# DLRM tower on one core: who issues and converts the head tables' loads, and a re-laid order of 96 moving units a block

## The reference

```python
e = jnp.stack([tbl_0[ids[:, 0]], ..., tbl_39[ids[:, 39]]], axis=1)   # 2048 x 40 x 64
vi, vj = x[:, i_idx, :], x[:, j_idx, :]                              # the 780 pairs i < j
z = jnp.einsum('bpe,bpe->bp', jnp.einsum('bpd,pde->bpe', vi, W), vj)
h = jnp.concatenate([z, dense_ctx], axis=1)                          # 780 + 16
h = jnp.maximum(h @ W_top1 + b_top1, 0.0)                            # 512
h = jnp.maximum(h @ W_top2 + b_top2, 0.0)                            # 256
y = h @ W_top3
```

## Time and profile before

| | before |
|---|---|
| median of 3 runs | 1236.23 us (1236.14 to 1239.3) |
| the profiled execution | 1235.82 us |
| its span, first to last instruction | 1233.9 us |
| busy in it: PE, DVE, ACT, POOL | 1189.6, 1064.7, 976.7, 778.2 us |
| VectorE products (units) | 800 |
| R units summed by V, A, P | 102, 234, 48 |
| mean DMA rate | 66 GB/s |

### The profile page before, as it was taken

One profiled execution on the slowest core, in us unless ns is written; L12 is line 12 of the kernel. 1 busy time (PEld: TensorE's weight loads), 2 busy tenths in 40 slices (PEclk: granted clock), 3 DMA queues, 4 the chain that ended last, 5 costly groups with the idle time before them and its releaser, 6 DMA issues.

```text
span 1233.9 us, 22918 instructions
## 1 busy us (share of the span) xinstructions
PE 1189.6 (96%) x5656; PEld 429.3 (35%) x5656; DVE 1064.7 (86%) x973; ACT 976.7 (79%) x7625; POOL 778.2 (63%) x1032
## 2 busy tenths in 40 slices
PE   4899998999999999999999999999999999999999
PEld 1332332333333333333333333433333334333333
DVE  4789999999987979999989979789989898989960
ACT  0149859999868889999959769999959687899971
POOL 7888882467765555787755656678766565545420
PEclk9999999999999999999999999999999999999999
DMA  4243222222222222222223222222222222212100
GB/s 152 72 143 71 69 69 55 59 72 68 71 63 60 64 61 69 69 67 68 68 64 77 62 58 64 62 64 67 69 63 69 59 68 64 61 48 54 55 5 1
DMA packets 65868, 80.92 MB, mean 66 GB/s; under 512 B 14772, under 2 KB 41396, under 8 KB 65608
## 3 DMA queue, kind: packets, MB, share of 16 engines
q1 hardware_dynamic: 44064, 55.14, 15.3%
q0 software_dynamic: 19456, 19.96, 9.2%
q10 hardware_dynamic: 2216, 4.36, 1.0%
HBM read 79.40 MB, written 0.01 MB: 64 GB/s over the span
## 4 chain that ended last, share of the span: by engine, by line
PE 91%; DVE 3%; ACTq 3%; issue 2%; ACT 1%; DVEq 0%
PE u_ps L921 31%; PE u_ps L917 28%; PE z_ps L938 16%; PE turn_ps L969 7%; PE turn_ps L889 3%; PE turn_ps L882 2%; PE turn_ps L979 2%; ACTq L1163 2%; PE u_ps L969 1%; DVE rprod_V L1056 1%; DVE rprod_A L1056 1%; DVE zb L1075 1%; ACTq L1161 1%; DVE fprod L1069 1%; PE u_ps L979 1%
## 5 line engine op out<-in xcount | busy, mean ns | idle before, releaser
L1118 ACT ACTIVATE rprod_A<-rprod_A 128x64 f32<-128x64 f32 x3744 | 895.8, 243 | 57.8 <-DVE rprod_A L1056 56.7
L826 POOL DMA_INDIRECT rows<-in_tbl,ids_all x608 | 576.0, 947 | 326.5 <-PE u_ps L921 114.3
L1118 ACT ACTIVATION_READ_ACCUMULATOR rprod_A<-rprod_A 128x1 f32 x3744 | 707.9, 189 | 0.1
L1069 DVE TENSOR_TENSOR fprod<-u_ps,x 128x1024 f32<-128x1024 f32 x416 | 492.9, 1214 | 36.1 <-PE u_ps L921 36.1
L921 PE MATMUL u_ps<-x,wf_ring 64*128 64x512 f32 x1664 | 428.5, 612 | 11.5 <-DVE rprod_V L1056 6.9
L917 PE MATMUL u_ps<-wr_ring,x 64*128 64x512 f32 x1536 | 394.8, 613 | 5.0 <-DVE rprod_V L1056 4.7
L1056 DVE TENSOR_TENSOR rprod_A<-u_ps,rows 128x1024 f32<-128x1024 f32 x234 | 281.8, 1216 | 71.4 <-PE u_ps L917 71.1
L921 PEld LDWEIGHTS u_ps<-x,wf_ring 64*128 64x128 f32 x1664 | 145.4, 185 | 242.8 <-issue 152.6
L917 PEld LDWEIGHTS u_ps<-wr_ring,x 64*128 64x128 f32 x1536 | 132.7, 186 | 221.7 <-issue 129.6
L938 PE MATMUL z_ps<-fprod,ones 128*32 128x512 f32 x1664 | 206.8, 598 | 0.0
L846 POOL TENSOR_TENSOR rprod_P<-rprod_P 128x512 f32<-128x512 f32 (+4 forms) x240 | 145.6, 607 | 77.1 <-DVE rprod_P L1056 61.4
(11 more groups left out here) (35 smaller groups left out, 187.4 us busy)
## 6 DMA issues: line engine op xcount, KB each, us to landing
wf_ring<-in_w_standing SPq DMA_DIRECT2D x208, 128.0 KB
wr_ring<-in_w_moving SPq DMA_DIRECT2D x96, 256.0 KB
rows<-in_tbl,ids_all POOLq DMA_INDIRECT x608, 2.5
mlp_sb<-in_mlp SPq DMA_DIRECT2D x1, 2308.0 KB, 9.8
mlp_sb<-in_tbl ACTq DMA_DIRECT2D x6, 250.0 KB
rows<-in_first_ids ACTq DMA_DIRECT2D x4, 250.0 KB
rprod_P<-in_first_ids ACTq DMA_DIRECT2D x4, 250.0 KB
mlp_sb<-in_tbl ACTq DMA_DIRECT2D x2, 312.5 KB
```

Source lines behind the costliest of these rows:

```text
L826: nc.gpsimd.indirect_dma_start(rows[:, v % ROW_SLOTS, s, par * DIM:(par + 1) * DIM], None, tables[f], bass.IndirectOffsetOnAxis(ap=ids_all ...
L1069: nc.vector.tensor_tensor(fprod[:, f % FPROD_SLOTS], u_ps[:, bank:bank + 2, :], other, ALU.mult).then_inc(prods_done, 1)
L1118: op = nc.scalar.activation(of[:, j, :], of[:, j, :], ACT.Copy, accum_out=sums_at(u, j, 1))
```

## The change

1. **Loads.** The loads of the 8 hot tables and of their ids go from ScalarE's queue to SP's. SP issues the ids of all gathers, then the loads of tables 0 to 3, then the first four chunks of standing weights, then tables 4 to 7, then the moving weights. The ids go to 128 partitions and not to 125; a table's load is cut into two, 112 and 13 partitions. Ids and tables have semaphores of their own.
2. **Ids as floats.** ScalarE converts each 128x512 ids tile in place from int32 to float32 (`convert_ids`, 8 instructions). VectorE's build waits for the converted ids and no longer for the table; TensorE waits for the table.
3. **The order.** Quads 2 and 3 of the fields have 5 and 7 moved columns and not 4 and 8 (still 24 chunks, 96 units a block). The costs and limits of the planner change. The turn of a chunk of row sums ("zr") may be placed within its own block, when its sums are done, and need not stand before layer 1 in the next one. What the planner makes of it: R units summed by V, A, P go from 102, 234, 48 to 89, 228, 67 (by block V: 33, 23, 24, 22 to 32, 25, 20, 12; P: 7, 12, 13, 16 to 11, 15, 17, 24). Block 0 takes its first P sum behind 126 of the 128 gathers of duos 4 to 19.

The core of the diff (the costs of the planner are numbers of a table; a line or two of it stands here):

```diff
-MOVED = [0, 4, 4, 8, 8]
+MOVED = [0, 4, 5, 7, 8]
+HOT_LOADS = [slice(0, 112), slice(112, 125)]
...
-LEAD, LEAST, ROWS_LEAD = 4, 1, 5
+LEAD, LEAST, ROWS_LEAD = 6, 1, 4
-A_MOST, P_MOST = 1.5, 1
+A_MOST, P_MOST = 1, 1
...
 def tail_of(b):
-    return ([("zr", b, c) for c in range(ZR)] + [("l1", b, m) for m in range(M1)] +
-            [("l2", b, m) for m in range(M2)] + [("l3", b, 0)])
+    return [("l1", b, m) for m in range(M1)] + [("l2", b, m) for m in range(M2)] + [("l3", b, 0)]
...
         for b in range(NB):
             base, f, r = DUOS * b, 0, 0
+            mlp += [("zr", b, c) for c in range(ZR)]
...
+            def load_table(h):
+                f, at = HOT_FIELDS[h], HOT_AT[h]
+                sp.dma_start(hot_ids[h].bitcast(I32),
+                             first_ids[h:h + 1, :].partition_broadcast(P)).then_inc(hot_ids_in[h], 16)
+                table = tables[f].rearrange("(p r) d -> p (r d)", p=HOT_PARTS)
+                for parts in HOT_LOADS:
+                    sp.dma_start(mlp_sb[parts, at:at + DIM * HOT_SPLIT[h]], table[parts, :]).then_inc(hot_in[h], 16)
+            for h in range(4):
+                load_table(h)
             for c in range(WF_SLOTS):
                 load_standing(c)
+            for h in range(4, 2 * HOT):
+                load_table(h)
...
-                            pe.wait_ge(hot_in[h], 2 * 16)
+                            pe.wait_ge(hot_in[h], 16 * len(HOT_LOADS))
...
-                    dve.wait_ge(hot_in[h], 2 * 16)
+                    dve.wait_ge(hot_ids_known, h + 1)
...
+            def convert_ids(n):
+                for h in range(2 * n, 2 * n + 2):
+                    act.wait_ge(hot_ids_in[h], 16)
+                    nc.scalar.copy(hot_ids[h], hot_ids[h].bitcast(I32)).then_inc(hot_ids_known, 1)
...
+                if v + 2 < HOT:
+                    convert_ids(v + 2)
...
-            for h, f in enumerate(HOT_FIELDS):
-                at = HOT_AT[h]
-                act.dma_start(hot_ids[h][0:HOT_PARTS, :],
-                              first_ids[h:h + 1, :].partition_broadcast(HOT_PARTS)).then_inc(hot_in[h], 16)
-                act.dma_start(tables_sb[:, at:at + DIM * HOT_SPLIT[h]],
-                              tables[f].rearrange("(p r) d -> p (r d)", p=HOT_PARTS)).then_inc(hot_in[h], 16)
+            for n in range(2):
+                convert_ids(n)
```

More of the change, by code:

```diff
@@ L198 @@
 T_GATHER, T_ROWS, T_FOLD = 1.25, 2.5, 3.3
-T_PACE, PACE_OVER, AHEAD_OF = 1.6, 4, 1.0
+T_PACE, PACE_OVER, AHEAD_OF = 1.6, 6, 1.0
 LAG_PE, LAG_DVE, LAG_ACT, LAG_POOL = 0.225, 0.15, 0.09, 0.08
 T_FIRST = 4.3
-T_HOT, T_BUILD, T_TABLE, T_TABLES = 0.423, 0.35, 5.5, 2.8
-LEAD, LEAST, ROWS_LEAD = 4, 1, 5
-STALL, GAP = 0.05, 0.2
+T_HOT, T_BUILD, T_TABLE, T_TABLES = 0.423, 0.35, 6.0, 1.6
+LEAD, LEAST, ROWS_LEAD = 6, 1, 4
+STALL, GAP = 0.05, 0.5
 MLP_GAP, MLP_PACE = 4, 14
-AHEAD, BEHIND = 2, 6
-A_MOST, P_MOST = 1.5, 1
+AHEAD, BEHIND = 1, 6
+A_MOST, P_MOST = 1, 1
 def tail_of(b):
-    return ([("zr", b, c) for c in range(ZR)] + [("l1", b, m) for m in range(M1)] +
-            [("l2", b, m) for m in range(M2)] + [("l3", b, 0)])
+    return [("l1", b, m) for m in range(M1)] + [("l2", b, m) for m in range(M2)] + [("l3", b, 0)]
 class Plan:
@@ L477, in step_ready @@
         if what == "zr":
+            if len(self.r_units) < NR * b + min(NR, SUBS * (P // FOLD) * (n + 1)):
+                return None
             for u in self.r_units:
@@ L564, in run @@
                     len(self.f_units) + 1 - FPROD_SLOTS >= NF * sums[0][0] + GROUP * sums[0][1])
-                must_step = mlp and any(ev[0] in ("zr", "l1") for ev in mlp) and sums and (
+                must_step = any(ev[0] in ("zr", "l1") and ev[1] < b for ev in mlp) and sums and (
                     sums[0][1] >= K_GROUPS * (Z_SPARE + 1) - 1)
@@ L592, in run @@
                     if sb == b - 1 and sg == GROUPS - 1:
-                        mlp = tail_of(sb)
+                        mlp[len(mlp) - ZR:len(mlp) - ZR] = tail_of(sb)
                 elif what == "duo":
@@ L613, in run @@
             self.do_sums(*s)
-        for ev in tail_of(NB - 1):
+        for ev in mlp + tail_of(NB - 1):
             self.do_step(ev)
@@ L691, in dlrm_tower @@
         hot_ids = [(rows[:, h, :, :].rearrange("p s c -> p (s c)") if h < 4
-                    else rprod["P"][:, (h - 4) // 2, (h - 4) % 2, :]).bitcast(I32) for h in range(2 * HOT)]
+                    else rprod["P"][:, (h - 4) // 2, (h - 4) % 2, :]) for h in range(2 * HOT)]
         y_row = h1_sb[0:1, 0, :]
@@ L706, in dlrm_tower @@
         hot_in = [sem(f"hot_in{h}") for h in range(2 * HOT)]
+        hot_ids_in = [sem(f"hot_ids_in{h}") for h in range(2 * HOT)]
+        hot_ids_known = sem("hot_ids_known")
         rows_known = sem("rows_known")
```

## The result

The changed kernel takes 1227.1 us (median of four runs, 1225.2 to 1228.4) and the kernel before 1236.3 beside it: a ratio of 0.9915, interval 0.9901 to 0.9928. That is 9.2 us faster, where 17.3 were forecast. The time lies inside the range of 1207 to 1230 and outside the forecast's own range of 1213 to 1224. The profiled execution took 1225.2 (span 1223.4), the quickest of the four. The other three took 1226.5 to 1228.4, at mean granted clocks of TensorE of 0.996, 0.994 and 0.994 where the profiled one had 0.997.

What follows compares the result with a forecast made beforehand. It took TensorE to bound the kernel, 91% of the chain of waits, with its idle time in the first 64 us. Head -13.5, row sums -1.1, end -2.7 gave -17.3, so 1219 us; own range 1213 to 1224, wider range 1207 to 1230.

Steps and rivals of the forecast that it cites:

- Head: loads: Table loads at the kernel's start: on SP's queue they run at 237 GB/s, so table 1 is there at 9.0 us.
- The slow bound: Table loads in the head at 143 GB/s: table 1 at 13 us, four us later, the head's gain only -9.5 us.
- Head: ScalarE: ScalarE in the head: its 16 load issues go, conversions of 0.59 us come, and the 5.25 us wait for a copy goes.
- Head: builds: VectorE's builds in the head stay at 0.53 us each, held up mutually with POOL; float ids bring nothing.
- The low end: Head with builds of 0.27 us: TensorE's own chain then decides, ending at 44.9 us, -16.2 us.
- Head: sum: The head ends at 47.6 us, by VectorE's chain, and not at 61.1: -13.5 us.
- Does block 0 follow?: Block 0 behind the head: gathers land before duos 7 and 11 are turned, so gathers were put at nothing.
- Row sums: VectorE's row sums: one fewer at 98 to 238 us, where a sum costs its whole 1.13 us; -1.1 us.
- the other twelve: The other twelve sums VectorE loses: put at nothing, bound 13.6 us to the good.
- the four rivals: Order gives more, 1209 (0.22); head half mended, 1223 to 1229 (0.13); loads still blocked, 1228 (0.06); POOL late, 1240 (0.04).
- rival 2: The head is only half mended, its loads coming at the slow rate: about 1223 to 1229 us, chance 0.13.
- The end: Before the last layer 1: two of three rounds of row-sum turns go, -2.7 us, or -1.1 at the least.

Runs made afterwards that it cites:

- head_load125: head with each hot table in one load of 125 partitions, not 112 and 13, and its ids on 125 partitions; 1228.3 us, ratio 0.9918 to the kernel before.
- head: The changed kernel's new head (loads, float ids) with the planner and order of the kernel before; 1223.9 us, ratio 0.9891 to the kernel before.
- head_short_pause: head with POOL's pause between block 0's gathers as a memset of 8 columns, not 256; 1220.7 us, ratio 0.9858 to the kernel before.
- mixed_again: Second run of mixed, on a chip of usual speed; 1218.1 us, ratio 0.9846 to the kernel before.
- replan: The changed kernel with one planner condition mended: a chunk turn is forced only by sums of the present block; 1222.6 us, ratio 0.9886 to the kernel before.
- zr2_later: The changed kernel with the third chunk turn of blocks 0 to 2 moved to just before the next turn; 1231.9 us, ratio 0.9959 to the kernel before.
- head_tail_again: Second run of head_tail, on a chip of usual speed; 1221.6 us, ratio 0.9871 to the kernel before.
- order: The kernel before with the changed kernel's planner, so the new order with the old head; 1240.5 us, ratio 1.0026 to the kernel before.
- head_tail: head with the last block's first two chunk turns placed among the units; on the slow chip alone, ratio 0.9931 to the kernel before there.
- head_int: head with integer ids and no conversions on ScalarE; on the slow chip alone, ratio 0.9956 to the kernel before there.
- mixed: replan with the planner's six old constants in block 0 alone; on the slow chip, ratio 1.0092 to the kernel before there.
- zr2_b0: The changed kernel with block 0's third chunk turn alone moved behind the block's last sums; slow chip alone, 1363.1 us, ratio 1.0228 to the kernel before.

## Why the forecast was right in sign and too large

1. **Head: loads.** Right in the rate, and not quite in what waits for what. Table 1 was to be there at 9.0, of which the 1 us for the end of a load has no row. A build waits for converted ids and no longer for the table: its ids are there by 8.54, and the second build starts at 9.18. The profile puts TensorE's first weight load from table 1, at 9.82, down to the table, so it was there by then; this cost nothing, as the builds set the pace. The slow bound, 143 GB/s and a table four us later, is what head_load125 measures: 141 GB/s, that weight load at 13.80 and not at head's 9.87, the second build 3.2 us later and the last layer 1 4.4.
2. **Head: ScalarE.** Right. A conversion takes 0.62 where 0.59 was taken, and the copy that came at 33.41 comes at 19.78.
3. **Head: builds.** Right in the term (0.54 for 0.53) and in its cause, POOL's pause. Float ids bring nothing at this pace: 18.74 us for 35 builds with int32 against 18.76. The Trainium skill (Advanced Engine Details and Errata, VectorE Performance Modes) names no type among the conditions of the two-port mode, and the trace agrees. The low end, TensorE's own chain to 44.9, is what head_short_pause reaches with 44.7.
4. **Head: sum.** 48.4 for 47.6, -12.7 us for -13.5. Short by 0.8, and all of it at the end: the products before the last two builds start at 43.97, as forecast (44.0). The last two builds take 1.09 us and not 0.87, and the last two steps (four matmuls) wait 1.39 us and take 1.46, so the head ends 1.1 us behind the last build where one step of 0.45 was put.
5. **Does block 0 follow?** Right. Duo 7 turns at 64.75 (64.0 forecast) and TensorE waits for gathers three times, by 1.2 us in all and 0.5 at most; head keeps the 12.7 to the end.
6. **Row sums.** This step failed, in block 0. One V sum fewer was to give 1.1 us, and "the other twelve" and the turns nothing. Block 0 lost 2.1 us in the changed kernel instead (3.2 in replan, with the same list there and a slow clock). I had compared counts over 100 units and not how the order around them falls. mixed_again shows that the planner's six constants for block 0 decide it: with them as before, block 0 loses nothing behind product 25. The single mechanism is open. The twelve sums in blocks 1 to 3 did bring little: from product 225 to 800 the changed kernel gains 2.2 us.
7. **What the sum left out.** Nothing in it priced the border of blocks. It had the turns earlier "among units where VectorE has the pace", and the order showed one directly behind the last unit whose row sums it needs. Price: 4.8 us, of which 1.9 is the slow clock (5.61 for 3.70); zr2_later, with the turn elsewhere, does not pay it. It is the largest missing term. None of the four rivals named it; rival 2's interval holds the time, but its cause (slow loads) was not there. That 1227.1 lies inside 1207 to 1230 is therefore partly luck: the width was given for other reasons.
8. **The end.** -2.6 for -2.7 in the rounds; the bound of -1.1 net, with the turns at 0.8 each, is closer to what head_tail_again shows, 1.5 net with 0.6 each.

The sum as measured in the profiled runs: -12.6 + 2.1 + 4.8 - 2.2 - 2.6 = -10.5, and the spans differ by 10.5. The medians give 9.2. The three slower runs have the lower mean clocks, so more slow clock is the likely reason for the difference; no trace of them is kept. Where the order has neither fault, in mixed_again, layer 1 is 17.7 us earlier and the kernel takes 1218.1, near the forecast's sum by slightly other terms: 13.0 by product 25, 0.1 in the rest of block 0, 1.9 in blocks 1 to 3 and 2.7 at the end. Its granted clock is 1.00 throughout, which also helps it.

## What to carry to other kernels

Price an order of instructions by its places and not by its counts: at each border ask of every instruction that needs a whole block's result how much work the engine that makes that result still has ahead of it, because everything queued behind the instruction waits too, and the clock can fall with it. Run the halves of a change apart first; head and order showed in two runs that the one gave more than the whole and the other cost. Where two engines' short instructions lengthen each other, shorten the one that does no work: the pause of 8 columns gave 3.8 us at the last layer 1, and the conversion of the ids cost about 1 at the first product.

## What the runs showed of the hardware that was not expected

- **One of the chips is much slower for this kernel.** On it the kernel before took 1332.5 us, and head_tail 0.9931, head_int 0.9956, mixed 1.0092 and zr2_b0 1.0228 of that. The head is the same there to 0.1 us (products 1 and 7 of head_tail against head), but between 60 and 200 us TensorE stands still again and again with nothing that the profile shows. TensorE, 90 to 240 us, head_tail there:

```profile
117.99 2.08 PE L951 MATMUL u_ps<-x,wf_ring 64*128 64x512 f32 x4 [11.71 <-issue]
...
143.93 2.08 PE L951 MATMUL u_ps<-x,wf_ring 64*128 64x512 f32 x4 [12.70 <-issue]
```

  By product 75 it has lost 72 us against head. All engines but POOL stand in these gaps. The cause stays open, and so does why the new orders lose more there than the old one; the changed kernel itself was not run there, and it may well be a loss.
- **The same program, the same wait, two clocks.** Before the last layer 1 TensorE waits 0.87 us in every profiled run on the other chips. In some (before, after, order, zr2_later, replan, mixed_again, head_tail_again) the 14 matmuls behind it take 6.25 us, in others (head, head_load125, head_short_pause) 7.75 to 7.95; in head the granted clock is 0.57 there:

```profile
1186.00:1190.00 4.00, 3.89 (x5) 1.63 (x6) 0.00 (x0) 0.00 (x0) 0.00 (x0) 0.57 0.00 0
1190.00:1194.00 4.00, 4.00 (x11) 1.81 (x10) 0.00 (x0) 0.00 (x0) 0.00 (x0) 1.00 0.00 0
```

  The three slow ones all have three rounds of turns before layer 1, each of the last two behind a wait of 0.68 us; of the profiled runs with one round none is slow. But the kernel before has three rounds and 6.25, so the rounds alone do not decide it. These 1.7 us are of the size by which the runs of one kernel differ (the kernel before: 1235.7 to 1239.0 on one chip). The start of that step leaves them out, and the table above has it; it still holds every fall of the clock further up, as in order and replan.
- A fall of the clock after a wait cost 1.9 us on four units here, and 2.8 on a layer's step (9.06 for 6.25), a third of the wait before it (5.75) and seven tenths (3.98).
